# Attention and expert kernel: new order of small pieces, a value product joint over 256 tokens, and a signal for each load

## What is computed

```python
x = x + xattn(layernorm(x), ctx, ctx)      # q = x@Wq + bq, k = ctx@Wk + bk, v = ctx@Wv + bv
#   scores = q.k / 4 ; attn = sparsemax(scores) = max(scores - tau, 0), sum = 1 ; out = (attn @ v) @ Wo + bo
x = x + ffn(layernorm(x))
#   hidden = square(relu(x @ w1[e])) ; expert_out = hidden @ w2[e] ; weighted by the two best gates; + shared expert
```

## Time and profile before

| | us |
|---|---|
| median of 3 runs | 865.37 |
| lowest, highest | 864.1, 870.45 |
| span of the profiled execution | 863.6 |
| PE busy in it | 768.4 (89%) |
| DVE busy | 606.6 (70%) |
| POOL busy | 518.4 (60%) |
| ACT busy | 461.1 (53%) |
| MAX8 of batch 0 starts | 27.99 |
| output add of batch 0 (L1100) starts | 179.16 |
| output adds of batches 12, 13, 14, 15 start | 741.38, 785.25, 827.27, 860.26 |

### The profile page before, as it was taken

One profiled execution on the slowest core, in us unless ns is written; L12 is line 12 of the kernel. 1 busy time (PEld: TensorE's weight loads), 2 busy tenths in 40 slices (PEclk: granted clock), 3 DMA queues, 4 the chain that ended last, 5 costly groups with the idle time before them and its releaser, 6 DMA issues.

```text
span 863.6 us, 15088 instructions
## 1 busy us (share of the span) xinstructions
PE 768.4 (89%) x5056; PEld 628.9 (73%) x5056; DVE 606.6 (70%) x1827; ACT 461.1 (53%) x794; POOL 518.4 (60%) x590
## 2 busy tenths in 40 slices
PE   1666449999999899999999999999999999899998
PEld 1544337877878787878788787877787888688877
DVE  1788977878687878777786877887877778742221
ACT  1545454656655566656566566656665656442321
POOL 2459585758666675757586766667575757541010
PEclk9958668999999999999999999999999999999999
DMA  8300001020202002020102020110202020202010
GB/s 254 124 7 14 8 12 51 13 66 5 75 1 74 9 14 62 13 68 16 62 5 74 6 74 2 50 32 14 62 13 68 3 62 2 61 2 62 2 62 12
DMA packets 37358, 34.88 MB, mean 40 GB/s; under 512 B 23153, under 2 KB 34078, under 8 KB 35230
## 3 DMA queue, kind: packets, MB, share of 16 engines
q1 hardware_dynamic: 34934, 28.88, 11.9%
q0 software_dynamic: 1248, 4.73, 1.6%
q10 hardware_dynamic: 1096, 0.29, 0.2%
HBM read 28.30 MB, written 4.33 MB: 38 GB/s over the span
## 4 chain that ended last, share of the span: by engine, by line
PE 41%; DVE 23%; POOL 11%; DMA 11%; issue 8%; ACT 3%; DVEq 1%; ACTq 0%; POOLq 0%
PE y_ps L816 14%; PE h_ps L803 11%; DVE fsum L947 8%; DMA sw_all<-sw_scratch 8%; POOL over L342 7%; PE m_ps L767 6%; PE s_ps L759 4%; PE m_ps L776 4%; DVE g L1092 3%; DVE fold_a L959 2%; ACT hid L577 2%; DMA sw_scratch<-swT 2%; DVE den L967 1%; DVE f_stats L895 1%; DVE ln_stats L895 1%
## 5 line engine op out<-in xcount | busy, mean ns | idle before, releaser
L342 POOL TENSOR_TENSOR over<-S,tau 128x1232 f32<-128x1232 f32 x128 | 286.5, 2249 | 201.3 <-DVE tau L977 198.8
L816 PE MATMUL y_ps<-w_sb,hid 128*128 128x256 f32 x1152 | 279.1, 385 | 23.0 <-ACT hid L577 22.9
L803 PE MATMUL h_ps<-x1nT,w_sb 128*128 128x256 f32 x1152 | 275.6, 382 | 0.0
L816 PEld LDWEIGHTS y_ps<-w_sb,hid 128*128 128x128 f32 x1152 | 211.6, 190 | 65.5 <-ACT hid L577 37.5
L803 PEld LDWEIGHTS h_ps<-x1nT,w_sb 128*128 128x128 f32 x1152 | 215.1, 191 | 30.5 <-issue 2.8
L577 ACT ACTIVATE hid<-g 128x512 f32<-128x512 f32 x144 | 89.9, 625 | 113.3 <-DVE g L1092 112.8
L947 DVE TENSOR_REDUCE fsum<-over 128x16 f32<-128x1232 f32 x96 | 137.0, 1427 | 16.2 <-POOL over L342 13.8
L1092 DVE SCALAR_TENSOR_TENSOR g<-h_ps,sw_all 128x512 f32<-128x512 f32 x128 | 87.5, 684 | 75.1 <-PE h_ps L803 43.0
L526 ACT ACTIVATE signs<-over 128x1232 bf16<-128x1232 f32 x96 | 115.1, 1225 | 22.9 <-POOL over L342 22.9
L923 DVE MAX8 top<-S 128x8 f32<-128x77 f32 x512 | 74.6, 223 | 3.3 <-ACT S L516 3.3
L342 POOL TENSOR_TENSOR attn<-S,tau 128x1232 f32<-128x1232 f32 x32 | 71.8, 2263 | 6.1 <-PE s_ps L759 5.8
(11 more groups left out here) (111 smaller groups left out, 941.9 us busy)
## 6 DMA issues: line engine op xcount, KB each, us to landing
sw_all<-sw_scratch SPq DMA_DIRECT2D x16, 1024.0 KB, 5.3
x_sb<-in_x SPq DMA_DIRECT2D x16, 256.0 KB, 2.7
w_sb<-in_w POOLq DMA_DIRECT2D x2, 2048.0 KB, 12.0
out_y<-wk_sb SPq DMA_DIRECT2D x16, 256.0 KB, 5.7
sw_all<-in_ctx SPq DMA_DIRECT2D x1, 1078.0 KB
v_block<-v_all SPq DMA_DIRECT2D x56, 9.6 KB
wk_sb<-in_wk SPq DMA_DIRECT2D x1, 256.0 KB
wv_sb<-in_wv SPq DMA_DIRECT2D x1, 256.0 KB
```

What stands on the lines that cost most here:

```text
L342: return pool.tensor_tensor(dst, S[:, p, t, :, 0:NK], tau[:, p, t].rearrange("p (h o) -> p h o", o=1).broadcast_to([P, NH, NK]), ALU.subtract)
L803: last = pe.matmul(h_ps[:, i % 2, c, :], w1_sb[:, e, k, c * P:(c + 1) * P], x1nT[:, p, k, :], start=(k == 0), stop=(k == KC - 1))
L816: last = pe.matmul(y_ps[:, t, :], hid[:, i % 2, c, t * P:(t + 1) * P], w2_sb[:, e, c, :], start=(i == 0 and t == 0 and c == 0), stop=(i == ...
```

## The change

The stages are cut into smaller functions and put in a new order on each engine, and the turns now run from b = -1. The experts of a batch start one turn earlier: `layer1(b - 2, 0)` opens turn b on PE, and the last two `layer2` follow in turn b+1. All four rounds of a batch stand in one turn. The two halves' value products are one: 17 matmuls of 256 columns, one eviction of 512 elements, for which `attnT` holds both halves. The count goes to a part of `s_ps` instead of `y_ps`. Each load has a semaphore of its own; SP issues x first and the expert weights last of its loads; ACT issues the first context rows; the initial increments of the semaphores are shared by POOL and PE. Line numbers in the diff's functions have moved: L342 becomes L344, L767 becomes L805, L803 L849, L816 L861, L1100 L1178.

The core of the diff (of the turns mostly the new text; the old one stands in the code above; the pieces of the pairs in turns -1 to 2 are left out):

```diff
-        o_done, o_taken = sig("o_done", T), sig("o_taken", T)
+        o_done, o_taken = sig("o_done"), sig("o_taken")
         count_done, count_taken = sig("count_done"), sig("count_taken")
...
@@ -235,12 +235,10 @@
 
 
 
-        def turns(eng, turn, first=None):
-            if first is not None:
-                first()
-            for b in range(NB + 3):
-                turn(b, b % 2, 1 - b % 2, new=b < NB, mid=1 <= b < NB + 1, late=2 <= b < NB + 2, old=b >= 3,
-                     ahead=b < NB - 1)
+        def turns(eng, turn):
+            for b in range(-1, NB + 3):
+                turn(b, b % 2, 1 - b % 2, ahead=b < NB - 1, new=0 <= b < NB, mid=0 <= b - 1 < NB, late=0 <= b - 2 < NB,
+                     old=b >= 3)
 
 
         @block.sync
...
+            sp.dma_start(wo_sb[:], chunked(wo)).then_inc(o_loaded, 16)
+            sp.dma_start(w1_sb[:, 0:E], w1.rearrange("e (k p) n -> p e k n", p=P)).then_inc(w_ffn, 16)
+            sp.dma_start(w1_sb[:, E], chunked(cfc)).then_inc(w_ffn, 16)
+            sp.dma_start(w2_sb[:, 0:E], w2.rearrange("e (k p) n -> p e k n", p=P)).then_inc(w_ffn, 16)
+            sp.dma_start(w2_sb[:, E], chunked(cproj)).then_inc(w_ffn, 16)
+            sp.dma_start(gate_sb[:], chunked(gate_w)).then_inc(w_ffn, 16)
+            sp.wait_ge(consts, N_CONSTS)
+            for b in range(NB + 2):
+                turn(b, b % 2, 1 - b % 2, new=b < NB - 2, mid=1 <= b < NB + 1, old=b >= 2)
             sp.wait_ge(out_stored.sem, out_stored.at(NB - 1))
 
 
         @block.gpsimd
         def _(pool):
...
-            for t, v in ((ones, 1.0), (neg_half_pow, -0.5), (exponents[:, 0:2 * T], 0.5), (exponents[:, 2 * T:], -0.5),
+            for t, v in ((neg_half_pow, -0.5), (ones, 1.0), (exponents[:, 0:2 * T], 0.5), (exponents[:, 2 * T:], -0.5),
                          (picked[:, :, 2 * E:], 1e-6)):
                 pool.memset(t[:], v).then_inc(consts, 1)
...
-            pool.dma_start(w2_sb[:, 0:E], w2.rearrange("e (k p) n -> p e k n", p=P)).then_inc(w_ffn, 16)
...
+                pool.sem_inc(s.sem, s.per)
             pool.wait_ge(consts, N_CONSTS)
 
...
-            def turn(b, p, q, new=False, mid=False, late=False, old=False, ahead=True):
+            def turn(b, p, q, ahead, new, mid, late, old):
+                if late:
+                    mid_subtract(b - 2, p, 0)
+                    mid_subtract(b - 2, p, 1)
+                    mid_tolerance(b - 2, p)
+                if mid:
+                    subtract(b - 1, q, 0, 0)
+                    subtract(b - 1, q, 0, 1)
+                    new_residual(b - 1, q)
+                if new:
+                    new_rstd(b)
+                if mid:
+                    subtract(b - 1, q, 1, 0)
+                    subtract(b - 1, q, 1, 1)
+                if late:
+                    late_rstd(b - 2)
                 if new:
                     new_keys(b)
...
+                    subtract(b - 1, q, 2, 0)
+                    subtract(b - 1, q, 2, 1)
                 if late:
                     late_pick(b - 2)
...
                     late_weight_roots(b - 2)
...
+                if mid:
+                    subtract(b - 1, q, 3, 0)
+                    subtract(b - 1, q, 3, 1)
+
+            turns(pool, turn)
...
+            act.dma_start(iota[:], iota_in).then_inc(iota_loaded, 16)
+            act.dma_start(bk_sb[:], bk).then_inc(k_loaded, 16)
+            act.dma_start(head_of[:], head_of_in).then_inc(head_loaded, 16)
+            act.dma_start(bq_sb[:], bq).then_inc(q_loaded, 16)
+            act.dma_start(bv_sb[:], row(bv, NK)).then_inc(v_loaded, 16)
+            act.dma_start(bo_sb[:], row(bo, P)).then_inc(o_loaded, 16)
+            act.dma_start(lb_sb[:], row(lb_bias, P)).then_inc(lb_loaded, 16)
+            act.wait_ge(iota_loaded, 16)
 
...
+            def late_pieces(m, t, i):
+                cols = slice(t * P, (t + 1) * P)
+                act.wait_ge(aT_done.sem, aT_done.at(m, SB * t + i + 1))
+                act.wait_ge(o_done.sem, o_done.at(m - 1))
+                if i < SB - 1:
+                    last = act.activation(attnT[:, 4 * i:4 * i + 4, cols],
+                                          s_ps[:, i, :].rearrange("p (h n) -> p h n", h=4), ACT.Copy)
+                else:
+                    act.activation(attnT[:, 4 * i, cols], s_ps[:, i, 0:P], ACT.Copy)
+                    last = act.activation(attnT[0:LAST, 4 * i + 1, cols], s_ps[0:LAST, i, P:2 * P], ACT.Copy)
+                last.then_inc(aT_taken.sem, 1)
+
+            def late_heads(m):
+                act.wait_ge(o_done.sem, o_done.at(m))
                 act.wait_ge(wo_done.sem, wo_done.at(m - 1))
-                act.activation(OT[:, :, t * P:(t + 1) * P], pair(t), ACT.Copy).then_inc(o_taken.sem, 1)
-
-            def late_turned(m, p):
+                act.activation(OT[:].rearrange("p k n -> p (k n)"), m_ps[:, 0, :], ACT.Copy).then_inc(o_taken.sem, 1)
+
+            def late_product(m):
+                for t in range(T):
+                    for i in range(SB):
+                        late_pieces(m, t, i)
+                late_heads(m)
...
+                if late:
+                    late_pieces(b - 2, 1, 1)
+                    late_pieces(b - 2, 1, 2)
+                    late_heads(b - 2)
+                if new:
+                    new_norm(b, p)
...
+                if mid:
+                    sign_or_relu(b - 1, q, 1, 0)
...
+                if mid:
+                    sign_or_relu(b - 1, q, 1, 1)
...
+                if mid:
+                    sign_or_relu(b - 1, q, 3, 0)
+                if old:
+                    old_square(b - 3, 7)
+                if mid:
+                    sign_or_relu(b - 1, q, 3, 1)
+                if new:
...
+                if mid:
+                    late_pieces(b - 1, 0, 0)
+                    late_pieces(b - 1, 0, 1)
+                    late_pieces(b - 1, 0, 2)
+                    late_pieces(b - 1, 1, 0)
...
+                    pe.wait_ge(s_taken.sem, s_taken.at(m + 1))
+                else:
+                    pe.wait_ge(aT_taken.sem, aT_taken.at(m - 1))
                 for side in (unsettled, below):
                     for t in range(T):
-                        last = pe.matmul(y_ps[0:1, 0, 0:1], side[:, t:t + 1], ones[:],
+                        last = pe.matmul(s_ps[0:1, SB - 1, 0:1], side[:, t:t + 1], ones[:],
                                          start=(side is unsettled and t == 0), stop=(side is below and t == T - 1))
                 last.then_inc(count_done.sem, 1)
 
...
+            def late_heads(m):
                 pe.wait_ge(v_placed[m // 2 % 2], 16 * len(PIECES) * (m // RING + 1))
-                pe.wait_ge(attn_checked.sem, attn_checked.at(m))
-                if new:
...
-                    for c in range(4 * i, min(4 * i + 4, CHUNKS)):
-                        rows = min(P, FLAT - c * P)
-                        last = pe.transpose(s_ps[0:rows, i, c % 4 * P:(c % 4 + 1) * P], flat[:, c * P:c * P + rows], ident[:])
-                    last.then_inc(aT_done.sem, 1)
+                pe.wait_ge(gate_chain.sem, gate_chain.at(m - 1, 1))
                 for i, blocks in enumerate(BY_BANK):
-                    pe.wait_ge(aT_taken.sem, aT_taken.at(m, SB * t + i + 1))
+                    pe.wait_ge(aT_taken.sem, aT_taken.at(m, SB + i + 1))
                     for c, a in blocks:
...
+            def late_output(m, t):
+                if m == 0:
+                    pe.wait_ge(o_loaded, 16 * 2)
+                pe.wait_ge(o_taken.sem, o_taken.at(m))
+                if t:
+                    pe.wait_ge(swT_taken.sem, swT_taken.at(m - 1))
+                for c in range(KC):
+                    last = pe.matmul(m_ps[:, t, 0:D], OT[:, c, t * P:(t + 1) * P], wo_sb[:, c, :],
...
+                if late:
+                    layer1(b - 2, p, 0)
...
+                if late:
+                    layer1(b - 2, p, 1)
...
+                if late:
+                    layer1(b - 2, p, 2)
+                if old:
+                    layer2(b - 3, 7)
+                    layer2(b - 3, 8)
...
+                if mid:
+                    late_unsettled(b - 1, b - 1 + 1 < NB)
...
+                if late:
+                    layer1(b - 2, p, 3)
+                if mid:
+                    late_pieces(b - 1, 0, 0, b - 1 + 1 < NB)
+                    late_pieces(b - 1, 0, 1, b - 1 + 1 < NB)
+                    late_pieces(b - 1, 0, 2, b - 1 + 1 < NB)
+                    late_pieces(b - 1, 1, 0, b - 1 + 1 < NB)
+                if late:
+                    layer1(b - 2, p, 4)
...
+                if mid:
+                    late_pieces(b - 1, 1, 1, b - 1 + 1 < NB)
+                    late_pieces(b - 1, 1, 2, b - 1 + 1 < NB)
+                    late_heads(b - 1)
...
+                if mid:
+                    late_output(b - 1, 0)
+                    late_output(b - 1, 1)
+                if late:
+                    layer2(b - 2, 0)
```

(93 more changed lines are left out.)

499 lines of the change are left out of this document (205 added, 294 removed).

## The result

| | before | after |
|---|---|---|
| median, us | 865.23 | 841.62 (838.46 to 845.02) |
| ratio, 95% interval | | 0.971 (0.967 to 0.976) |
| span of the profiled execution | 863.6 | 836.7 |
| first MAX8 starts | 27.99 | 23.23 (forecast 17) |
| final tau of batches 0 and 1 | | 63.30, 107.09 (forecast 57, 103) |

A forecast was written before the change was run, and what follows sets the result against it. PE was taken as nearly the bound, a second ring of POOL, ACT and DVE beside it. 103 + 14 x 46.0 - 1.5 + 42.0 + 35.5 + 3.4 = 826.4 span, so 828 us median; range 809 to 850.

The forecast's parts named there:

- then from xn to MAX8: Start: 10.0 us from xn to first MAX8, less 2.4 of keys; first MAX8 at 17, 11 earlier.
- Steady turn, by PE: PE's work in a turn: 44.4 after a 0.6 product saving, plus 0.8 bare wait and 0.7 stalls, 45.9 us.
- bare wait: PE, ahead of the product by Wo: waits uncovered for the one eviction of 512 elements, 0.8 us with hand-over.
- The 3.1: Value product on PE with the Trainium skill's factor of 2.38: 3.1 us, giving a turn of 46.8 and 839.
- Steady turn, by the ring: POOL, ACT and DVE from one final tau to the next: 44.6, with Wo's product 1.2 late 45.8 us.
- count, `s_ps` in the place of `y_ps` ... cost nothing of their own: they lie under PE's groups: Steady turn on PE: these, shared semaphore increments and two-half `attnT` are hidden; uncovered, each below 0.6 a turn.
- the first rival: Steady turns: PE's stalls close wholly and the ring keeps up, 44.8 a turn, 811 us; chance 0.15.
- 0.9 for gates and layer-norm steps that do not fit beside the subtractions: Ring's rounds 1 and 2 in a steady turn: 0.9 us added to 17.9 for these steps.
- Ring and PE catch on each other: Steady turns: in-order ACT and DVE make rounds wait for a late product; 47.3 a turn, 846 us; chance 0.25.
- PE's stalls close wholly: Steady turns: PE's stalls vanish and the ring keeps up, 44.8 a turn, 811 us; chance 0.15.
- the slower one: Steady turns: DVE waits for a count behind five PE groups, 8.7 us; two uncovered give 49.5, 877; chance 0.05.
- The rival drawn from the rule on DMAs of several engines: Start: 4.6 MB of expert weights let loose at once make first loads late; 839 us, within the 0.25 rival.

The follow-up runs named there:

- e3: Changed kernel, but all engines again wait for all attention loads before first work and GpSimd issues the expert weights; 853.2 us, ratio 0.986.
- e2: Changed kernel with VectorE's first layer-norm statistics (batch 0) ahead of the first key sums; 841.6 us, ratio 0.972.
- e7: e1 with both the edit of e5 (lean later) and that of e6 (verdict with a scalar); 820.1 us, ratio 0.947.
- e1: Changed kernel, but SyncE issues the load of x ahead of the 25 small placements of values; 838.9 us, ratio 0.970.
- e5: e1 with the first `lean` moved behind the folds of the round before; 837.7 us, ratio 0.966.
- e11: Changed kernel with only e6's verdict edit, x still loaded late; 826.0 us, ratio 0.951.
- e6: e1 with the verdict reading one tensor and the tolerance as a per-partition scalar, in four small instructions; 818.2 us, ratio 0.943.
- e12: e7 plus e2's statistics edit, with OT's eviction in two of 256 columns and the first tokens' Wo product in the other bank; 812.4 us, ratio 0.935.
- e10: e7 with the joint value product cut into two of 128 columns back to back, one eviction kept; 828.4 us, ratio 0.955.
- e4: Changed kernel with the joint value product cut into two of 128 columns back to back, one eviction kept; 842.9 us, ratio 0.974.

## Why the prediction was right or wrong

The direction was right, and 841.6 lies in the range of 809 to 850; of the forecast gain of 37 us 24 came. The sum was 826.4 for a span that measured 836.7. By its own terms:

| term | forecast | measured | difference |
|---|---|---|---|
| final tau of batch 1 | 103 | 107.09 | +4.1 |
| 14 turns | 644.0 | 759.89 - 107.09 = 652.8 | +8.8 |
| end | 79.4 | 836.7 - 759.89 = 76.8 | -2.6 |

**Start.** Work started at 6.23, near the 5 to 6 of the forecast, and 5.1 earlier than before; the first MAX8 came 4.8 earlier instead of 11. The 11.1 of e3 is no support for the 11, as its loads land later than those of before. The step that failed is "then from xn to MAX8": it took xn as ready when x was, and did not follow VectorE's list, in which the statistics of x stand behind the key sums. xn came at 14.25, where the forecast needs it near 10. That is worth 3.7 at MAX8 (e2). The rest is the late `bk_sb` (0.80) and queries at the lower clock (3.75 us against 1.99 for such eight in the trace of before).

**Batches 0 and 1.** From MAX8 to the final tau 40.1 us, forecast 40. The next ring took 43.8, forecast 46. So the ring without experts was priced 0.8 too high (44.6), and the 1.4 for the product at the low clock didn't show in it.

**Steady turn, by PE.** Forecast 45.9 = 44.4 + 0.8 + 0.7. Where TensorE does set the turn, in e7, it is 44.03 + 0.70 + 0.15 and rounding, 44.92. The bare wait was right (0.70 for 0.8), the product close (2.38 for 2.2, a saving of 2.8 - 2.38 = 0.4 for 0.6; against two back to back, 2.52, it is only 0.14). The 3.1 that the prediction worked out beside it was not seen. 44.98 - 0.4 = 44.58 is just what e1 shows; the other 0.5 down to 44.03 are those that left with VectorE's stalls.

**Steady turn, by the ring.** Forecast 45.8. The wait that set the turn was in no term: the verdict standing still for 1.5 us behind GpSimd's subtraction, worth 1.34 a turn and 17.6 us from e5 to e7, where it is the only difference. From after, where it comes in every second turn, to e11 it is 1.09 and 15.6, with a stalled `lean` that went along. The sentence "count, `s_ps` in the place of `y_ps` ... cost nothing of their own: they lie under PE's groups" is the one that failed: the count is made from the verdict, which moved from a moment in which GpSimd was idle into its subtraction, and TensorE waited for it uncovered, at more than the 0.6 that the sentence allows. With the stalls gone (e11) the turn is 45.47 and the median 826.0, close to the forecast's 46.0 and 828; with x early too (e6, e7) 44.92 and 818 to 820, between the forecast and the first rival's 811. The term "0.9 for gates and layer-norm steps that do not fit beside the subtractions" was the place for it, but it priced these as work, not as instructions that stop.

**The rivals.** "Ring and PE catch on each other" describes what happened, at 46.56 instead of 47.3; the places it named (eviction of OT ahead of the sign, residual ahead of the sum) were not it in the changed kernel. That the median of 841.6 lies as near as 4 to that rival's 846 is partly chance: its turns were shorter than it has them, and the start was 6.2 later than forecast. "PE's stalls close wholly" is what e6 and e12 turn the kernel into. For the slower one (the count read behind five groups) nothing spoke: VectorE waited for the count 2.0 us in all, in 4 waits between 250 and 750 us. The rival drawn from the rule on DMAs of several engines was not seen: the first matmul starts at 6.23, with the expert weights let loose.

**What would show it.** The adds' interval and the first add were off as above. The broadcast's wait was gone, the OT wait there. GpSimd waited for tau 3 times a turn (33 waits in 11 turns), not four. "A DVE wait above 2 us" was named as a sign of error for count or residual; the one that came, 4.2 to 4.6 for x, was of another tile, because the 25 placements ahead of it on SyncE were not counted. It cost 2.9 us here between the final taus of batches 1 and 15, and 6.1 where the stall was gone.

**The gain.** Of the 26.9 us of span 6.5 are there at the first output add (forecast 14), 3.5 come in the twelve turns (10 = 12 x 0.85), and 16.9 behind them: the last turns take 37.3, 40.1 and 24.6 us where they took 43.9, 42.0 and 33.0. That part, the turn without experts that is gone, was forecast at about 13.

## To carry to other kernels

When a change moves small instructions, look at what the neighbouring engine runs at the new moment, not only at what the instruction waits for: one of 0.15 us took 1.63 for that alone, and set the turn. Every later shift asks for the same look: 0.14 us more in a product moved `fold_a` behind another instruction and cost 0.42 on top, and a start 3.7 us earlier was lost to two such stalls. An edit that takes one stall away can take a second along (e6), so what each is worth is read from a pair of runs that differ in it alone. A group of the page whose mean duration changed without an edit is the first thing to follow. And a late transfer that measures as next to nothing may be hidden by a larger stall; try it again once that is gone (2.9 became 6.1 us).

## What the runs showed of the hardware

- VectorE's instruction with two SBUF inputs, started during GpSimd's two-tensor subtraction of 2.25 us, ended with it: 1.63 and 2.19 us instead of 0.15 and 0.20. With one tensor and a per-partition scalar four instructions took 0.2 each in the same stretch (e6), and a gate multiply whose second tensor is in PSUM was not held (38 of 38 in after). GpSimd's subtraction was hardly longer (2.25 to 2.29). Where both started within 0.02 us of each other, GpSimd's `k_diag` took 1.06 instead of 0.71 and VectorE's `fold_a` its usual 0.48 (e7).
- SyncE took 0.85 us for each of 25 small placements, 21.20 together; what stands behind them in the list waits.
- 34 matmuls of 256 columns into four groups of 32 output partitions took 2.38 us, 68 of 128 columns 2.52 (e10) to 2.67 (e4).
